# Three written-out orders instead of one for a fused attention kernel, with its loads placed anew

## The chip, the cores and the metric

One Trainium2 chip, one core of it. The metric is the device time of one execution in microseconds (us); lower is better. TensorE (PE) does the matmuls, VectorE (DVE) reductions and element work, ScalarE (ACT) exponentials and copies, GpSimd (POOL) small element work, and SyncE (SP) issues nearly all DMAs.

## The reference, cut to what matters

Four sequences of 1024 rows, 256 wide, with a context of 154 rows each:

```python
x = attention(ln1(x), ln1(x), Wq1, Wkv1, Wo1, bo1) + x        # 16 heads of 16, over 1024 keys
x = attention(ln2(x), context, Wq2, Wkv2, Wo2, bo2) + x       # 16 heads, over 154 keys
x = geglu_ff(ln3(x), Wff1, bff1, Wff2, bff2) + x              # 256 -> 2*1024 -> 256
# second layer: one head, 256 wide, over the 154 context rows
out = softmax((x@Wq.T+bq) @ (ctx@Wk.T+bk).T) @ (ctx@Wv.T+bv) + x
```

## The kernel before, in words

The 4096 rows are cut into NCH = 16 chunks of 256. A chunk goes through five stages, each in another iteration of one software pipeline over n: **pre** (layer norm, q, k and v, letter p, 8 steps) in iteration n = chunk; the self-attention itself (letters M, Q, T, S, V, O, o, u) of chunk n-5; **mid** (Wo1, residual, layer norm, q2; letter m, 9 steps) of chunk n-6; **cross** (the attention over the context; letter c, 36 steps) of chunk n-7; **last** (Wo2, feed-forward, second layer; letter l, 26 steps) of chunk n-8. Iterations 0 to 3 are a head of their own; then run() goes over n = 4 to 20, and walk_end does what is left (mid and cross of chunk 15, cross of 14, last of 13, 14 and 15) by END_ORDER.

Within an iteration the order of all work is a string, ORDER, of 248 letters. Every engine walks the same string by walk() and takes from each letter what that letter's work has for it; so each engine's queue is in the string's order, and engines meet only at semaphores. A letter whose stage doesn't exist in the iteration (l before n = 8, p from n = 16 on) is passed over. SP, too, is only held by its own waits and may be far ahead of TensorE in the string.

The letters that matter here:

- S is half a step of scores (2 matmuls, then one exponential on ACT), V is two steps of probabilities times values (16 matmul records), M is one matmul of 512 columns whose row maximum VectorE reduces; 64, 16 and 64 of them in an iteration. After 16 M's a unit (4 heads) is complete: Q reduces the pairs on VectorE, T turns the result on TensorE (waiting for Q), makes the shift of the exponentials on VectorE, and SP stores it. Units of M run two ahead of those of S. I write T3 for the fourth T, c35 for the last of the 36 steps of c, counting from 0.
- o stores an attention output (SP), u loads the stacks of q and k of a later unit (SP), O copies an output from PSUM (ACT).
- c1 to c12 are maxima of the cross-attention (3 matmuls or 1, and one reduction on VectorE each), c13 turns them, c14 stores the shift (SP), c16 to c35 are scores, exponentials and values. At c25 and c35 SP stores half of its output to DRAM (store_o2).
- The four letters d, i, e, f prepare the last stage of the *next* iteration: d waits until c35's store has landed and loads the softmax denominators (den_c); i inverts them on VectorE, which waits for that load, and SP stores the inverses; e loads the output sums (oT2); f waits for the inverses' landing and loads them broadcast (den2). VectorE multiplies the two in l2, and TensorE projects in l3.
- x loads the q2 stack of the next cross stage; in every fourth iteration (n = 10, 14, 18) k2 and v2 too. TensorE first needs it at c1 of the next iteration.

```python
sp.wait_ge(c_ost, (o + 1) * 32)                  # d, on SP
load_den(1, o2_rows(o))
...
dve.wait_ge(c_den[which], (o + 1) * 16)          # i, on VectorE
nc.vector.reciprocal(den_c[which][:, :], den_c[which][:, :]).then_inc(c_rd[which], 1)
```

In walk_end the letters are c and d (cross of chunks 14 and 15), m (mid of 15), x, y, z (last of 13, 14, 15), and loads: q (the cross stack for d), i j k l (the four load steps for y), r s t u (the same for z).

Of the kernel before, what the change touches and what calls it, by code (L numbers as in the profile page):

```python
# [21 lines left out]
NCH = B * S // CH  # L22
# [34 lines left out]
MAX_LAG, ATT_LAG, MID_LAG, CROSS_LAG, LAST_LAG = 4, 5, 6, 7, 8  # L57
# [3 lines left out]
LEAD = 2  # L61


ORDER = (
    "cMMSSMlSoMSMcSSMlcMSlcVScMM"
    "SmcllVuMSSMucMSMmSSoMmMScSMlQcVTcp"
    "SpcSMMlcSOVMcSMSlSMScVcMpS"
    "SMlVMSpMlcMSucSpMcSMlScMpSMSlcMVM"
    "ScQlSpSTpcScmcMMlcVMcSMlSMcSMOSclmMu"
    "SVVMSMSmcMlSoSMmMScMSlMmMMQSlcVTlcMM"  # L70
    "SlcSMSMOVSMcmSMlSclMSMVxcSdM"
    "SMlSMSMVSMSMSMSiMQeflSVoTVOl"
)


CT_STEPS = 3
# [12 lines left out]
def setup_steps(n, slot):  # L89

    return SETUP_AT.count(SLOTS * (n - MAX_LAG) + slot)
# [4 lines left out]
END_CROSS = dict(c=NCH - 2, d=NCH - 1)  # L96
END_LAST = dict(x=NCH - 3, y=NCH - 2, z=NCH - 1)
END_LOADS = dict(q="d", i="y", j="y", k="y", l="y", r="z", s="z", t="z", u="z")
END_ORDER = "mcxcccccxxccxccmxcmcxccxccccmmcccxccmxccmxxcmxccmcxxcccccxccxqxkxxixddxdddxdjddlxdxdddyydxdddyyxdddyzdddyyddddydddddyddddyyydryyyzystyzzzyyzyyzyuzzzzzzzzzzzzzyzzyyyzzzz"


def in_end(o):
# [26 lines left out]
def xattn_kernel(nc, t, out):  # L129

    ctx = ExitStack()
    with ctx:
# [308 lines left out]
        def walk(n, flags, setup, pre, mid, cross, last, work):  # L441


            has_pre, has_max, has_att, has_mid, has_cross, has_last = flags
            chains = dict(
                p=pre(n) if has_pre else None, m=mid(n - MID_LAG, has_pre) if has_mid else None,
                c=cross(n - CROSS_LAG) if has_cross else None, l=last(n - LAST_LAG) if has_last else None)
            seen = dict.fromkeys(ORDER, 0)
            for letter in ORDER:
                k = seen[letter]  # L450
                seen[letter] += 1
                if letter in work:
                    work[letter](k)
                elif letter in chains and chains[letter] is not None:
                    next(chains[letter])
                if letter == "S" and k % 2:
                    for _ in range(setup_steps(n, k // 2)):
                        next(setup)
            assert all(next(chain, None) is None for chain in chains.values() if chain is not None)

        def walk_end(mid, cross, last, loads=lambda letter: None):
# [4 lines left out]
            chains["m"] = mid(END_MID, False)  # L466
            for letter in END_ORDER:
                if letter in END_LOADS:
# [9 lines left out]
        def _(sp):  # L478
# [266 lines left out]
            def body(n, u, flags, att_before, after):  # L745
# [27 lines left out]
                def for_last(step):  # L773
# [3 lines left out]
                    return load  # L777

                walk(n, flags, setup_work, pre, mid, cross, last, dict(
                    T=store_shift, o=store_unit, u=load_unit, x=load_next_cross, d=for_last(load_last_den),  # L780
                    i=for_last(store_last_inv), e=for_last(load_last), f=for_last(load_last_inv)))
# [19 lines left out]
        def _(pool):  # L801
# [119 lines left out]
            def body(n, u, flags, att_before, after):  # L921
                walk(n, flags, setup_work, pre, mid, cross, last_by(1 - u), {})
# [8 lines left out]
        def _(act):  # L931
# [185 lines left out]
            def body(n, u, flags, att_before, after):  # L1117
                def exp_tile(k):
                    if not flags[2]:
                        return  # L1120
                    step, pair = SLOTS * (n - ATT_LAG) + k // 2, k % 2
                    act.wait_ge(g_s, 2 * step + pair + 1)
                    if step >= PR:
                        act.wait_ge(g_av, step - PR + 1)
                    nc.scalar.activation(probs[:, step % PR, 2 * pair:2 * pair + 2, :].rearrange("p j q -> p (j q)"),  # L1125
                                         ps_s[pair][:, :], ACT.Exp, scale=SCALE).then_inc(g_e, 1)

                def o_copy(k):
                    if not flags[2]:
                        return  # L1130
                    unit = HG * (n - ATT_LAG) + k
                    act.wait_ge(g_av, (unit + 1) * KT)
                    act.wait_ge(g_ost[unit % 2], unit // 2 * 16)
                    nc.scalar.copy(o_sb[:, unit % 2, :], ps_o[:, 0:CH]).then_inc(g_o, 1)

                walk(n, flags, setup_work, pre_by(flags[3]), mid, cross_by(not flags[2]), last, dict(
                    S=exp_tile, O=o_copy))
# [618 lines left out]
```

## Time and profile before

| | |
|---|---|
| median of 3 runs | 1776.59 us (1768.93 to 1783.04) |
| the profiled execution | 1771.07 us |
| its span, first to last instruction | 1769.3 us |
| mean granted clock of TensorE in it | 0.964 |
| TensorE, VectorE, ScalarE busy | 91%, 63%, 56% |
| iterations n = 5 to 20 | 96.5 us to 1592.8 us of the span |
| walk_end | 1592.8 us to 1769.3 us |

A busy TensorE is not one at its peak: a record of 128x256 lasts longer than the time until the next one may start. All times below are from the profiled execution.

### The profile page before, as it was taken

What the parts mean: (1) busy time and instruction counts of PE and PEld (TensorE: products, weight loads), DVE (VectorE), ACT (ScalarE), POOL (GpSimd) and SP (SyncE); (2) the same over time, 40 slices, a digit from 0 to 9 for tenths busy, and PEclk for the clock granted to TensorE, in tenths of its full rate; (3) what the DMA queues carried; (4) which work ended last, traced back from release to release, by engine and by line L of the source; (5) the groups of instructions that cost most, each with busy time, mean ns of one, the idle gap of its engine ahead of it and who ended that gap; (6) DMA issues with size and microseconds to landing.
All of it is one profiled execution on the core that took longest, in us unless ns stands there. A gap on an engine that the chain in (4) does not pass through costs nothing.

```text
span 1769.3 us, 33823 instructions
## 1 busy us (share of the span) xinstructions
PE 1610.6 (91%) x12897; PEld 1027.3 (58%) x12897; DVE 1109.2 (63%) x2221; ACT 988.1 (56%) x2024; POOL 264.9 (15%) x344
## 2 busy tenths in 40 slices
PE   6799999998999899998999899998999899896777
PEld 5444445564757566564756566564656556565566
DVE  4466786757676585857677585857676575824332
ACT  3246667565656466565656565565656556563232
POOL 5200312111111020121111021101010010101000
PEclk9989999999999999999999999999999999998788
DMA  6904243345131312445131321535030412221200
GB/s 186 223 23 132 60 87 82 82 88 122 43 85 52 66 59 62 97 85 117 51 83 50 62 60 55 104 58 116 18 83 26 79 38 48 59 43 46 56 25 13
DMA packets 171647, 129.37 MB, mean 73 GB/s; under 512 B 40751, under 2 KB 161885, under 8 KB 171229
## 3 DMA queue, kind: packets, MB, share of 16 engines
q1 hardware_dynamic: 171421, 127.19, 30.1%
q8 instruction: 102, 1.67, 0.4%
q14 instruction: 60, 0.49, 0.1%
q10 hardware_dynamic: 64, 0.02, 0.0%
HBM read 78.92 MB, written 47.71 MB: 72 GB/s over the span
## 4 chain that ended last, share of the span: by engine, by line
PE 63%; DVE 17%; DMA 10%; issue 3%; ACT 3%; SPq 3%; POOL 0%; DVEq 0%; POOLq 0%; ACTq 0%
PE ps_last L1620 10%; PE ps_max L1675 9%; PE ps_o L1709 9%; PE ps_s L1697 8%; DVE mxh L1346 7%; PE ps_last L1629 6%; DMA o_s<-o_sb 5%; PE ps_pre L1484 4%; PE ps_pre L1492 3%; PE ps_cross L1588 3%; DVE mx L1271 3%; PE ps_cross L1574 2%; DMA den_c<-o_s 2%; DMA den<-o_s 1%; DVE th L1303 1%
## 5 line engine op out<-in xcount | busy, mean ns | idle before, releaser
L1346 DVE TENSOR_REDUCE mxh<-ps_max 128x1 f32<-128x512 f32 x1024 | 661.1, 681 | 195.0 <-PE ps_max L1675 192.6
L1125 ACT ACTIVATE probs<-ps_s 128x512 f32<-128x512 f32 x1024 | 580.8, 598 | 302.4 <-PE ps_s L1697 278.7
L1675 PE MATMUL ps_max<-kst,qst 96*128 96x512 bf16 x1024 | 386.0, 393 | 21.3 <-DVE mxh L1346 11.7
L1697 PE MATMUL ps_s<-qst,kst 98*128 98x256 bf16 x2048 | 386.1, 277 | 6.7 <-ACT probs L1125 3.8
L1709 PE MATMUL ps_o<-probs,vg 128*17 128x256 f32 x4096 | 271.9, 387 | 0.0
L1697 PEld LDWEIGHTS ps_s<-qst,kst 98*128 98x128 bf16 x2048 | 176.7, 99 | 163.8 <-ACT probs L1125 72.6
L1675 PEld LDWEIGHTS ps_max<-kst,qst 96*128 96x128 bf16 x1024 | 96.0, 98 | 159.2 <-DVE mxh L1346 88.8
L1303 DVE SCALAR_TENSOR_TENSOR th<-th,gb 128x256 f32<-128x256 f32 x128 | 67.3, 526 | 178.7 <-ACT gb L1097 178.6
L1709 PEld LDWEIGHTS ps_o<-probs,vg 128*17 128x17 f32 x4096 | 96.5, 97 | 108.3 <-issue 42.0
L1066 ACT ACTIVATE probs<-ps_cross 77x512 f32<-77x512 f32 x224 | 132.6, 592 | 44.2 <-PE ps_cross L1574 44.0
L1620 PE MATMUL ps_last<-y_hi,wff_hi 128*128 128x256 f32 x448 | 141.1, 315 | 7.9 <-DVE hT L1306 7.9
L1620 PE MATMUL ps_last<-y_lo,wff_hi 128*128 128x256 f32 x448 | 126.4, 282 | 0.0
L1620 PE MATMUL ps_last<-y_hi,wff_lo 128*128 128x256 f32 x448 | 125.8, 281 | 0.0
L1629 PE MATMUL ps_last<-wff,hT 128*128 128x256 f32 x480 | 112.8, 380 | 2.0 <-DVE hT L1306 2.0
L1095 ACT ACTIVATE th<-ps_last,b_tanh 128x256 f32<-128x256 f32 x112 | 53.0, 473 | 98.4 <-PE ps_last L1620 97.3
L1620 PEld LDWEIGHTS ps_last<-y_hi,wff_hi 128*128 128x128 f32 x448 | 84.8, 189 | 22.1 <-DVE hT L1306 14.9
L863 POOL TENSOR_TENSOR qk_f<-qk_f,qk_parts 128x512 f32<-128x512 f32 x40 | 46.3, 1158 | 330.3 <-ACT qk_f L1033 167.1
L1629 PEld LDWEIGHTS ps_last<-wff,hT 128*128 128x128 f32 x480 | 87.9, 190 | 13.1 <-DVE hT L1306 2.6
L1574 PE MATMUL ps_cross<-q2st,k2st 98*77 98x256 bf16 x448 | 86.6, 274 | 8.4 <-ACT probs L1066 4.9
L854 POOL TENSOR_SCALAR ve<-mv 128x2 f32<-128x2 f32 x34 | 7.8, 230 | 557.6 <-DVE mv L1209 557.6
L1620 PEld LDWEIGHTS ps_last<-y_lo,wff_hi 128*128 128x128 f32 x448 | 85.0, 190 | 1.0
L1620 PEld LDWEIGHTS ps_last<-y_hi,wff_lo 128*128 128x128 f32 x448 | 85.1, 190 | 0.0
(265 smaller groups left out, 2013.0 us busy)
## 6 DMA issues: line engine op xcount, KB each, us to landing
parts_s<-qk_parts SPq DMA_DIRECT2D x28, 384.0 KB, 3.8
o_s<-o_sb SPq DMA_DIRECT2D x64, 128.0 KB, 2.8
o_s<-o_sb SPq DMA_DIRECT2D x32, 256.0 KB, 3.7
oT<-o_s SPq DMA_DIRECT2D x62, 128.0 KB
den<-o_s SPq DMA_DIRECT2D x62, 128.0 KB
kst<-parts_s SPq DMA_DIRECT2D x16, 384.0 KB, 5.0
kst<-parts_s SPq DMA_DIRECT2D x48, 128.0 KB, 5.9
qst<-parts_s SPq DMA_DIRECT2D x64, 96.0 KB, 2.2
```

The source lines that it names most:

```text
L1066: nc.scalar.activation(probs2[:, h % PR2, :], cross_banks[spare][h % 2][0:CT, :], ACT.Exp, scale=SCALE).then_inc(c_e, 1)
L1125: nc.scalar.activation(probs[:, step % PR, 2 * pair:2 * pair + 2, :].rearrange("p j q -> p (j q)"), ps_s[pair][:, :], ACT.Exp, scale=SCALE ...
L1271: nc.vector.tensor_reduce(mx2[:, h0:h0 + nh, i], cross_max_banks[spare][f % 2][:, 0:nh * CTX].rearrange("p (h n) -> p h n", h=nh), AX_X, A ...
L1303: nc.vector.scalar_tensor_tensor(th[:, m % 2, :], th[:, m % 2, :], 1.0, gb[:, m % 2, :], ALU.add, ALU.mult).then_inc(c_gt, 1)
L1346: nc.vector.tensor_reduce(mxh[:, i // 2, i % 2:i % 2 + 1], ps_max[i % 2][:, :], AX_X, ALU.max).then_inc(g_mx, 1)
L1484: last = mm(bank[:, m * CH:(m + 1) * CH], w[:, k, m * P:(m + 1) * P], y[:, k, :], start=(k == 0), stop=(k == KD - 1))
L1574: last = mm(cross_banks[spare][h % 2][0:CT, a * CH:(a + 1) * CH], k2st[:, at, a * CT:(a + 1) * CT], q2st[:, at, :], start=True, stop=True)
L1620: last = mm(last_banks(o)[m % 2][:, part * CH:(part + 1) * CH], wff1[w][:, k, cols_], y3[y][:, k, :], start=(i == 0), stop=(i == len(terms ...
L1629: last = mm(bank_[:, i * D:(i + 1) * D], hTs[e][:, m, i * P:(i + 1) * P], wff2[:, m, :], start=(m == 0), stop=(m == FM - 1))
L1675: mm(ps_max[i % 2][:, :], qst[0:ROWS, h, q * P:(q + 1) * P], kst[0:ROWS, h, k * 512:(k + 1) * 512], start=True, stop=True).then_inc(g_mt, 1)
L1697: last = mm(ps_s[pair][:, j * CH:(j + 1) * CH], kst[:, h, kt * P:(kt + 1) * P], qst[:, h, :], start=True, stop=True)
L1709: last = mm(ps_o[j * W:j * W + VW, 0:CH], vg[:, g, kt, j * VW:(j + 1) * VW], probs[:, step % PR, j, :], start=(kt == 0), stop=(kt == KT - ...
```

## The change

The one string becomes three: EARLY for n = 4 to 7 (no last stage yet), STEADY for n = 8 to 15 (all stages), LATE for n = 16 to 20 (no pre stage). Each holds the same letters as often as ORDER did, in another order. END_ORDER has the same letters in another order. No instruction is added or removed.

```diff
-ORDER = (
-    "cMMSSMlSoMSMcSSMlcMSlcVScMM"
...
-    "SlcSMSMOVSMcmSMlSclMSMVxcSdM"
-    "SMlSMSMVSMSMSMSiMQeflSVoTVOl"
+EARLY = (
+    "SSMMSMSMMSMSMSMcSVMo"
...
+    "SMlllllcMSmMMcVcSMOSMcmSMSdMlSVlSM"
+    "SlMVMSoSMMoSSMSMMQSSOlVlxTlielflVlll"
+STEADY = (
+    "lMMMSMcSMSMSMScScSMSMc"
...
+    "SclMMVVMMcSmlMSMlMSMclMMlQScSmVTcSSMcmMcl"
+    "SSMVMScSMOlSMmMlcMoSlMSMVSMM"
+    "SVSdMSMSMxSMQSlSSVioTVOefl"
+LATE = (
+    "MMlSSoMSMSMSMSMMSSMcccMl"
...
+    "SScmcMSSMVMmMSlcMSSMlOclSMVMMd"
+    "SxSMlMSSMVMSMlSMSieQVSlfTOoV"
+def order_of(n):
+
+    return EARLY if n < LAST_LAG else STEADY if n < NCH else LATE
-END_ORDER = "mcxcccccxxccxccmxcmcxccxccccmmcccxccmxccmxxcmxccmcxxcccccxccxqxkxxixddxdddxdjddlxdxdddyydxdddyyxdddyzdddyyddddydddddyddddyyydryyyzystyzzzyyzyyzyuzzzzzzzzzzzzzyzzyyyzzzz"
+END_ORDER = "cmcccccccxcxccxccccxcmcxmcxcccxcccccmcmmxxymccxmmxccxzdcxcyqxccxcxxxxxidddddxdjddxddddkdxxldxddyddddyxyddddddddyddydddzdydryyyysytyyzyyzzyyuzyzyzzzzzzzzyzzzzzyzyzyyzzzz"
-            seen = dict.fromkeys(ORDER, 0)
-            for letter in ORDER:
+            seen = dict.fromkeys(order_of(n), 0)
+            for letter in order_of(n):
```

## Rows read from the trace of the kernel before

**Rows 1.** The page: busy time by engine, and TensorE's granted clock in 40 slices.
```profile
PE 1610.6 (91%) x12897; PEld 1027.3 (58%) x12897; DVE 1109.2 (63%) x2221; ACT 988.1 (56%) x2024; POOL 264.9 (15%) x344
...
PEclk9989999999999999999999999999999999998788
```

**Rows 2.** Busy time by stretch: iterations 7, 10, 11, 18 and walk_end; length first.
```profile
core 0: us, PE busy (x) PEld busy (x) DVE busy (x) ACT busy (x) POOL busy (x), PEclk, DMA share, GB/s
...
238.80:314.60 75.80, 70.98 (x630) 37.33 (x629) 54.43 (x107) 50.75 (x100) 13.43 (x17) 0.99 0.27 71
...
514.70:618.60 103.90, 95.45 (x799) 61.92 (x798) 68.63 (x138) 60.41 (x124) 15.77 (x21) 0.98 0.28 67
618.60:716.00 97.40, 94.61 (x799) 62.18 (x798) 67.49 (x138) 60.53 (x124) 16.02 (x21) 0.99 0.23 61
...
1311.60:1411.70 100.10, 90.55 (x770) 56.80 (x769) 64.94 (x132) 56.73 (x117) 9.01 (x13) 0.97 0.26 56
...
1592.80:1769.30 176.50, 134.01 (x815) 102.71 (x814) 60.85 (x135) 53.28 (x121) 16.67 (x25) 0.81 0.13 35
```

**Rows 3.** Who waited for whom, TensorE, 303 to 1506 us: total, times, longest.
```profile
PE ps_max L1683 <- DVE mxq L1354: 40.5, 24, 5.4
```

**Rows 4.** The same view, within iteration 11 (619 to 700 us).
```profile
PE ps_max L1683 <- DVE mxq L1354: 0.8, 1, 0.8
```

**Rows 5.** Timeline of all engines at the end of iteration 10: start, length, idle before.
```profile
612.39 0.59 SPq L616 DMA_DIRECT2D den_c<-o_s  x1
614.45 0.35 DVE L1229 RECIPROCAL den_c<-den_c 128x32 f32<-128x32 f32 x1 [7.03 <-DMA den_c<-o_s]
...
615.39 0.17 DVE L1354 TENSOR_REDUCE mxq<-mxh 128x8 f32<-128x16 f32 x1
...
615.61 0.38 PE L1683 MATMUL ps_max<-ident,mxq 128*8 128x128 f32 x1 [5.40 <-DVE mxq L1354]
```

**Rows 6.** Timeline of SP's issues, ends of iterations 10 and 11.
```profile
599.18 0.33 SPq L660 DMA_DIRECT2D q2st<-q_s  x1
...
603.37 0.39 SPq L696 DMA_DIRECT2D o_s<-o_sb  x1
...
702.62 0.33 SPq L660 DMA_DIRECT2D q2st<-q_s  x1
702.99 2.10 SPq L667 DMA_DIRECT2D q2st<-q_s  x3
705.56 0.38 SPq L696 DMA_DIRECT2D o_s<-o_sb  x1
711.00 0.59 SPq L616 DMA_DIRECT2D den_c<-o_s  x1
```

**Rows 7.** DMA issues: count, KB each, median us from issue to landing.
```profile
o_s<-o_sb SPq DMA_DIRECT2D x64, 128.0 KB, 2.8
o_s<-o_sb SPq DMA_DIRECT2D x32, 256.0 KB, 3.7
...
q2st<-q_s SPq DMA_DIRECT2D x48, 128.0 KB, 5.9
```

**Rows 8.** The chain that ended last, iteration 15 and its end: start, length, what.
```profile
1085.49 0.44 PE ps_s L1697 x4
...
1092.01 1.73 PE ps_last L1629 x8
...
1103.97 0.99 PE ps_o L1709 x16
...
1106.29 4.82 DMA o_s<-o_sb
...
1111.13 2.16 DMA den_c<-o_s
...
1117.33 4.58 DMA den<-o_s
```

**Rows 9.** Busy time by stretch: the first 20 us of iteration 15.
```profile
1019.70:1039.70 20.00, 18.01 (x163) 9.98 (x161) 19.69 (x43) 11.19 (x21) 5.84 (x10) 0.99 0.31 91
```

**Rows 10.** Who waited for whom, TensorE, walk_end (1592.8 to 1769.3 us).
```profile
PE ps_last L1492 <- DVE oT L1234: 6.8, 2, 4.8
...
PE ps_s L1574 <- DMA q2st<-sh_lo: 2.4, 1, 2.4
PE ps_cross L1561 <- DVE mx L1271: 2.1, 1, 2.1
```

More of the change, by code:

```diff
@@ L61 @@
 LEAD = 2
-ORDER = (
-    "cMMSSMlSoMSMcSSMlcMSlcVScMM"
[L66 to L70, printed above, removed]
-    "SlcSMSMOVSMcmSMlSclMSMVxcSdM"
-    "SMlSMSMVSMSMSMSiMQeflSVoTVOl"
-)
+EARLY = (
+    "SSMMSMSMMSMSMSMcSVMo"
+    "SMSMSccSccMScMVMSumcSMMmQScmc"
+    "SVTpcSScuMpMScOVSMScVpSSMcoMcV"
+    "ScMpMSMSMpMcMSSMupMcSMVcMSSMcppQcTVOlc"
+    "SlmMcSMclSMllScMMScSMMcSSmMcV"
+    "SMmScMSMVMScMSMSmlMlulllcSMQVTcS"
+    "SMlllllcMSmMMcVcSMOSMcmSMSdMlSVlSM"
+    "SlMVMSoSMMoSSMSMMQSSOlVlxTlielflVlll"
+)
+STEADY = (
+    "lMMMSMcSMSMSMScScSMSMc"
+    "SlcMVoclSMcMSucSlMMlSVSSmMMSQc"
+    "SVTSlcSMcMlcmVScMMSSmOpplSoSMpcccV"
+    "SMSlSVpMMlSMuMcpScSMMlcpMMlVMMScQSlcpTc"
+    "SSpmcuMSSMclcSMVcSSmMulScOMM"
+    "SclMMVVMMcSmlMSMlMSMclMMlQScSmVTcSSMcmMcl"
+    "SSMVMScSMOlSMmMlcMoSlMSMVSMM"
+    "SVSdMSMSMxSMQSlSSVioTVOefl"
+)
+LATE = (
+    "MMlSSoMSMSMSMSMMSSMcccMl"
+    "SMcluVScMSMclMcMSlVSSMVcQmScST"
+    "SlccSMSoMlSScVMcMSOlScmVMMSlMcVM"
+    "SSlcScMmSSppMSMpcMplpcpSMMppcSl"
+    "SuMcMVQlcSTcSScmMMlcVMMSOuSclSuSc"
+    "SMMSVlmMcMlMMmScSlSMMSVMcMmSoMlMQcSlVTcM"
+    "SScmcMSSMVMmMSlcMSSMlOclSMVMMd"
+    "SxSMlMSSMVMSMlSMSieQVSlfTOoV"
+)
+def order_of(n):
+    return EARLY if n < LAST_LAG else STEADY if n < NCH else LATE
 CT_STEPS = 3
```

## The prediction

> **What bounds the kernel now.** I read the page first: TensorE is busy 91% of the span, VectorE 63%, and the granted clock is full except in the last four slices [rows 1]. So the bound is TensorE's queue and what holds it up, and the prize is its idle time, some 159 us of 1769.3. Then I cut the span at the first S of each iteration and read busy time by stretch. Iterations with all stages last 103.9 and 97.4 us with the same work and nearly the same busy TensorE (95.5 and 94.6), in turns, even ones longer; LATE-type iteration 18 has 100.1 against 90.6 busy [rows 2]. The reader is to see that the difference is waiting, and that it alternates. The view of waits names it: T, which turns the maxima, waits for Q on VectorE, 40.5 us in 24 waits, the longest 5.4 [rows 3]. No other wait of TensorE in that stretch holds 6 us in all.
>
> These are two kinds. Twelve are the T0 of iterations 8 to 19, 0.8 us each [rows 4], because Q0 stands just ahead of T0 behind VectorE's backlog: 12 x 0.8 = 9.7. The other 30.8 us are T3 at the iteration's end (the same view at each of the twelve ends gives 2.5, 1.2, 5.4, 0.5, 3.3, 0.2, 4.8, none, 3.8, 1.4, 5.2, 0.5 for iterations 8 to 19, and 2.0 for 7). The timeline of iteration 10 says why: VectorE idles 7.03 us in i, which waits for den_c; Q3 is behind i, so it comes at 615.39, and T3 behind that with 5.40 idle [rows 5]. And i is late because of SP's queue: x's ten loads start at 599.18, c35's store is behind them at 603.37, d may issue only when that store has landed, at 612.39, nine microseconds on [rows 5, 6]. In iteration 11, with four loads ahead (702.62), the store takes 705.56 to 711.00, 5.4 us [rows 6]. That is the alternation, in part: ten loads in 10, 14 and 18, the stacks of k of a new sequence in 8, 12 and 16.
>
> **The ends of iterations, STEADY.** Two moves. First, d stands ahead of x, so c35's store no longer has loads ahead of it. Second, i stands behind Q3 and V14, directly ahead of T3, and d to i is longer.
>
> PE time of a letter, from the chain: two S are 0.44, so S (and M) is 0.22; V is 0.99; an eight-record step of l is 1.73 [rows 8]. From the start of c35 to i, ORDER has 8 S, 7 M, a V, l23 and c35: 15 x 0.22 + 0.99 + 0.44 + 0.95 = 5.7 us. STEADY has 11 S, 9 M, 3 V, l23, l24 and c35: 4.4 + 3.0 + 0.4 + 1.7 + 1.0 = 10.5 us. The chain needs c35 0.95, the ACT copy 0.4, the store's landing, den_c's 2.16 with issue [rows 8] and 0.4 for the gaps. The store alone has no row of its own; bounds are 2.8 (128 KB stores) and 4.82 (iteration 15, four loads ahead) [rows 7, 8]; the median of all 256 KB stores is 3.7 [rows 7], half of them with loads ahead, and I take 3.2. Sum 7.1 us, at most 8.7, under 10.5. So i doesn't wait, and even if it did, Q3 is already done: what is late next would be M0 of the next iteration, which needs T3's shift from VectorE. T3 to M0 is one V (0.99) against 1.0 us for the turn and two small VectorE operations, even. All T3 waits of 8 to 15 go: 2.5 + 1.2 + 5.4 + 0.5 + 3.3 + 0.2 + 4.8 + 0 = 18.
>
> **LATE and EARLY.** In LATE i is ahead of Q3 but c35 to i is 9 M, 8 S, 2 V, l23, l24 and c35, 8.9 us against 7.1: 1.8 us of slack, and nil with the upper bound. T3 waits of 16 to 19 are 3.8 + 1.4 + 5.2 + 0.5 = 11, but Q3 to T3 is now V, S and no l24, 1.2 us, and I leave 0.5 each: -9. The order is also made for the missing p: iteration 18 has 9.6 us not busy, 4.4 with T3's 5.2 taken off, where ORDER bunches S, M and c after p's letters drop out. I take -1 for each of five, bounds +1 and -2: -5. In EARLY, iteration 7's T3 wait of 2.0 goes, because i is behind T3. For the rest of 4 to 7 VectorE is the tight engine (54.4 busy of 75.8 with TensorE at 71.0 [rows 2]) and I see no gain there, -2 in all, bounds +3 and -6.
>
> **What the moves cost.** (1) x is now issued after d, thus after the landing of c35's store: about 0.95 + 0.4 + 3.2 + 0.7 = 5.3 us after c35's start. Four loads are there 2 + 5.9 us after the first issue [rows 7], 13.2 after c35; TensorE reaches the next c1 after 11.6 (to the end) and 2.6, so 14.2 us in STEADY, 14.8 in LATE. Covered by 1 us. The ten loads of 10, 14 and 18 have no landing row that I quote but took up the queue from 599.18 to about 611 (the store behind them landed by 612.39 [rows 5, 6]): 11 to 13 us, so 16.3 to 18.3, 2 to 4 us late for c1, three times, less what iterations are longer than their pure PE time (6 us, so half a microsecond in this stretch): +6, bounds 0 and +12. (2) The inverses' store stands behind x's loads, and SP has o3 and T3's shift store ahead of e and f. f is issued some 5 us after T3 and takes 4.58 [rows 8], 9.7; l2 comes at 1.2 + 6.3 us of PE time, stretched by VectorE, about 8.3. In the first 20 us of an iteration VectorE is busy 19.69 [rows 9], so a wait in its queue costs its full length: +1 each for eight. But before, f landed at 1121.9 (1117.33 + 4.58), 5.7 us into iteration 16, with l2 already waiting, so the difference may be nil. I book 0, bounds +8 and -8. (3) That first stretch holds the same reductions in STEADY as in ORDER (12 of c and as many M, within two), so it stays at its 20 us. (4) u1 moves from before S12 to behind the first unit, so SP no longer stands there with T0's shift and m's loads behind it; nobody waits for these now, and the gain is nil.
>
> One rule of the skill speaks against (1) and (2). Rows 6 show the store of 256 KB take 9.0 us behind ten loads and 5.4 behind four. The Trainium skill, "DMA: Bandwidth & Descriptors", section "Queues, rings and completion order", says that an issuing engine has one ring on each DMA engine and that its descriptors are consumed in ring order, so whatever is put behind x's loads waits for them; the trace agrees. By that rule the change doesn't remove the queueing but hands it from den_c's path to that of the inverses, which is the second rival below.
>
> **walk_end**, 176.5 us with TensorE at 134.0 busy and a mean clock of 0.81 [rows 2]. The letters take the same PE time. x3 waited 4.8 us for x's inverses (the longest of L1492's 6.8 [rows 10]); END_ORDER now has c8 to c12 ahead of it, which fill that wait, and the turn c13 follows at once instead of behind two stalls of 2.1 and 2.4 [rows 10]. The first exponentials of cross 14 come some 8 us earlier, of which I count half, because afterwards c21 to c25 stand alone and go at ACT's pace. The load q is ahead of c35's store instead of behind it (1.9 us wait at d1), and y3 is behind d16 to d20 (1.9). z3 has 15 us behind d35 rather than 9 (2.0). Against that, d13 to d16 has lost y3 as its cover (+2), and heads 5 to 8 of d are no longer mixed with the feed-forward (+2). Sum -4 - 1.9 - 1.9 - 2.0 + 4 = -6; with a little less time at half clock, -8. Bounds +4 and -22.
>
> **The sum**, against the profiled execution's 1771.07 (span 1769.3 and 1.8 around it): -18 - 9 - 5 - 2 + 6 - 8 = -36, so 1735. The median shown is 5.5 us above that execution, inside a spread of 14; I put the forecast at 1736.
>
> **The clock** is the one place where a rule gives another result. In this trace it falls to half (1.2 GHz) for one or two short spells right behind the long T3 waits, in iterations that then last no longer: iteration 11 begins so and has 97.4 us [rows 2], and VectorE bounds that stretch anyway [rows 9]. So I book nothing for it in the main loop.
>
> **The rivals.**
> A. *Less idle also gives back clock time.* If the spells at half clock behind the T3 waits (some 37 us in seven) cost what TensorE loses in them, half, then 19 us more: 1717. Against it: odd iterations, which begin with the spell, are the short ones. The Trainium skill, "TensorE: Matmul & The Clock Gate", names as penalty throttled time times one minus the ratio, which is this half; the trace of iteration 11 speaks against it. A better walk_end (-22) gives the same place.
> B. *The wait moves to f and x.* VectorE waits at l2, or TensorE at c1, 1.3 us in each of 13 iterations instead of nil: +17 and 1753. For it: both slacks are about a microsecond, and VectorE is full there. Decides: f's landing against l2.
> C. *Slower.* If c35's store still takes its 4.8 to 5.4 us, x is issued 2 us later and lands 1 to 2 us after c1 each time, 6 us after it in 10, 14 and 18, and the inverses' path is behind those loads, so l2 stalls by 3 more: (2 + 1.5) x 10 + 9 x 3 = 62 against 42 of gains, 1791. It decides from a store of about 5 us on. Against it: nothing stands ahead of that store now but small ones.
> D. *The strings of their own do nothing*: STEADY alone, -18 + 4, 1757.
>
> **Chances.** Forecast (1725 to 1748) 0.57, A 0.14, B 0.15, D 0.09, C 0.05. The range holds A's upper part, B and D: 1710 to 1764. Within 1% of 1776.6, 1758.8 to 1794.4, is what a measurement of this kernel tells from no change. Faster: the forecast, A, most of B, half of D, 0.86, less some for unseen stalls: 0.84. Same 0.12, slower 0.04.
>
> **What would show it.** The profile after should have L1683's wait down from 40.5 to some 12 to 15 us; d's issue (L616) ahead of q2st's (L660) and some 3 us after c35's store; iterations 8 to 15 at 96 to 99 us without alternation, 16 to 19 at 92 to 95; walk_end at 165 to 172. A new row "PE ps_cross L1556 <- DMA q2st" would be cost (1), more time in "DVE oT L1234 <- DMA den" cost (2), and either above 15 us makes the forecast wrong upwards; iterations of 94 us without a spell at half clock, downwards.

## The result, and the profile after

The changed kernel takes 1709.53 us (median of 4 runs, 1707.72 to 1712.48), against 1776.09 before (median of 4, one more than the table ahead of the prediction had); the ratio is 0.9627, with a 95% interval of 0.9586 to 0.9668. Run again beside the kernel before (a_again, below) it was 1709.47 and 0.9649 (0.9623 to 0.9675). The forecast was 1736, and its range ended at 1710. The direction held and the main waits went as described; the size was short by 26 us between forecast and median, by 23 between the 36 us booked and the 58.6 between the two profiles.

The page of the profiled execution (1712.48 us, span 1710.7), against [rows 1]:

```profile
PE 1609.0 (94%) x12897; PEld 1019.8 (60%) x12897; DVE 1120.2 (65%) x2221; ACT 996.5 (58%) x2024; POOL 269.4 (16%) x344
...
PEclk9989999999999999999999999999999999997789
```

TensorE is busy for nearly the same time, 1609.0 us against 1610.6; 57.0 of the 58.6 us of span that went were its idle time. By stretch, with the same columns as [rows 2]: iterations 7, 10, 11, 18, 19 and walk_end.

```profile
236.60:310.30 73.70, 70.75 (x636) 37.72 (x633) 55.32 (x108) 51.32 (x100) 13.45 (x17) 1.00 0.37 82
504.40:601.10 96.70, 94.67 (x799) 61.49 (x798) 68.90 (x138) 61.11 (x124) 16.59 (x21) 1.00 0.28 67
601.10:697.80 96.70, 94.67 (x799) 61.48 (x798) 68.90 (x138) 61.10 (x124) 16.20 (x21) 1.00 0.26 67
...
1272.60:1366.20 93.60, 90.27 (x770) 56.53 (x769) 65.68 (x132) 57.05 (x118) 9.05 (x13) 1.00 0.22 54
1366.20:1460.50 94.30, 90.36 (x771) 56.61 (x770) 65.87 (x132) 57.15 (x118) 9.06 (x13) 1.00 0.23 56
1546.60:1710.70 164.10, 137.02 (x800) 101.60 (x798) 61.10 (x132) 53.65 (x121) 17.21 (x25) 0.81 0.15 39
```

Iterations 10 and 11 are alike now, 96.7 us, where they were 103.9 and 97.4, and the clock is at 1.00. The last S ends at 1546.8, so walk_end proper is 163.9 us. Cut the same way all along, the time went here:

| | before | after | gained | booked |
|---|---|---|---|---|
| up to the end of iteration 7 | 314.6 | 310.3 | 4.3 | 2 |
| iterations 8 to 15 | 801.6 | 773.5 | 28.1 | 18, less 4 of the 6 for x |
| iterations 16 to 20 | 476.6 | 463.0 | 13.6 | 14, less 2 of the 6 |
| walk_end | 176.5 | 163.9 | 12.6 | 8 |

Who waited for whom, TensorE, 301 to 1460 us, to be set beside [rows 3]: T's wait was 40.5 us in 24 and is 1.1 in 4. The prediction's own sign for it was 12 to 15 us, because it took the T0 waits (0.8 us each) to stay; they are all but gone too.

```profile
PE ps_last L1647 <- DVE hT L1333: 7.0, 16, 0.6
PE ps_max L1702 <- DVE mxh L1373: 6.1, 16, 0.6
...
PE ps_max L1710 <- DVE mxq L1381: 1.1, 4, 0.3
```

SP's issues at the end of iteration 10, beside [rows 5, 6] (L723 is c35's store, L643 d, L687 to L703 x, L647 the inverses' store, L656 f). These are nine loads, four of q2, four of k2 and one of v2; the prediction says ten, which is a miscount:

```profile
588.72 0.38 SPq L723 DMA_DIRECT2D o_s<-o_sb  x1
...
590.91 0.59 SPq L643 DMA_DIRECT2D den_c<-o_s  x1
591.60 0.53 SPq L687 DMA_DIRECT2D q2st<-q_s  x1
...
596.19 0.39 SPq L703 DMA_DIRECT2D v<-v_s  x1
598.39 0.61 SPq L647 DMA_DIRECT2D o_s<-den_c  x1
...
603.51 1.19 SPq L656 DMA_DIRECT2D den<-o_s  x2
```

The store lands 2.2 us after its issue (588.72 to 590.91), where it took 9.0; the median of the 32 such stores fell from 3.7 [rows 7] to:

```profile
o_s<-o_sb SPq DMA_DIRECT2D x32, 256.0 KB, 2.2
```

And the inverses' store now is the one behind the nine loads: issued at 598.39, it lets f go at 603.51, 5.1 us later. The queueing was handed on, as the prediction said it might be (its second rival). What it costs is the subject of half of the experiments.

### The profile page after: what moved, and what is told of

Its sections match the earlier page's. It is cut to its first block, busy times and chain, and to the rows that moved or that the text cites. A ratio compares the mean times of both kernels' runs of the same rounds, so it can differ in the third digit from the quotient of the medians.

```text
span 1710.7 us, 33819 instructions
## 1 busy us (share of the span) xinstructions
PE 1609.0 (94%) x12897; PEld 1019.8 (60%) x12897; DVE 1120.2 (65%) x2221; ACT 996.5 (58%) x2024; POOL 269.4 (16%) x344
## 4 chain that ended last, share of the span: by engine, by line
PE 71%; DVE 18%; ACT 5%; issue 3%; DMA 2%; SPq 1%; POOL 0%; DVEq 0%; ACTq 0%; POOLq 0%
PE ps_o L1736 11%; PE ps_max L1702 10%; PE ps_last L1647 9%; PE ps_s L1724 9%; DVE mxh L1373 8%; PE ps_last L1656 6%; PE ps_cross L1615 4%; PE ps_pre L1511 3%; PE ps_pre L1519 3%; DVE mx L1298 3%; PE ps_cross L1601 2%; PE ps_last L1685 2%; DVE th L1330 1%; ACT probs L1152 1%; PE ps_last L1519 1%
## 5 line engine op out<-in xcount | busy, mean ns | idle before, releaser
L1702 PE MATMUL ps_max<-kst,qst 96*128 96x512 bf16 x1024 | 363.4, 385 | 21.5 <-DVE mxh L1373 15.2
L1724 PE MATMUL ps_s<-qst,kst 98*128 98x256 bf16 x2048 | 371.6, 274 | 6.5 <-ACT probs L1152 4.9
L1724 PEld LDWEIGHTS ps_s<-qst,kst 98*128 98x128 bf16 x2048 | 171.7, 98 | 155.7 <-ACT probs L1152 57.9
L1736 PEld LDWEIGHTS ps_o<-probs,vg 128*17 128x17 f32 x4096 | 94.1, 96 | 112.2 <-issue 48.3
```

The source lines that it names most:

```text
L1702: mm(ps_max[i % 2][:, :], qst[0:ROWS, h, q * P:(q + 1) * P], kst[0:ROWS, h, k * 512:(k + 1) * 512], start=True, stop=True).then_inc(g_mt, 1)
L1724: last = mm(ps_s[pair][:, j * CH:(j + 1) * CH], kst[:, h, kt * P:(kt + 1) * P], qst[:, h, :], start=True, stop=True)
L1736: last = mm(ps_o[j * W:j * W + VW, 0:CH], vg[:, g, kt, j * VW:(j + 1) * VW], probs[:, step % PR, j, :], start=(kt == 0), stop=(kt == KT - ...
```

## The experiments

Times are beside runs of the kernel before on the same chip, as ratios with 95% intervals; "the changed kernel" is 0.9627 and 0.9649 by this measure. A thousandth is 1.8 us. Single executions vary: 31 of the kernel before on one chip lie between 1758.1 and 1779.8 us, and in the profiles with the old END_ORDER walk_end alone takes 173.0 to 184.9 us. So iterations are compared by stretch.

### One letter, or two, in the old string

**b_x**: x behind d, nothing else.

```diff
-    "SlcSMSMOVSMcmSMlSclMSMVxcSdM"
+    "SlcSMSMOVSMcmSMlSclMSMVcSdxM"
```

> The kernel before with one letter moved: x (the loads of the next cross stage) stands directly behind d instead of ahead of c35. Theory Q (the wait at T3 is queueing: x's loads ahead of c35's store): the store lands in 2.2 to 3.2 us instead of 5.4 to 9, den_c is there about 7 us after c35, i stands 5.7 us of TensorE's time behind c35 and waits 1 us or so, and the T waits of 40.5 us fall to 13 to 18; time 22 to 32 us less. Theory L (what counts is that i stands ahead of Q3): the wait at T3 stays at 2 us or more an iteration, time 0 to 10 us less.

Measured: 0.9953 (0.9926 to 0.998), 8 to 9 us less. Theory Q is right about the wait and wrong about the time, which falls into Theory L's range. T3 never waits; the 10.6 us left are T0's. But (waits of TensorE, 301 to 1600 us):

```profile
PE ps_cross L1556 <- DVE mx L1271: 13.2, 12, 2.4
PE ps_max L1683 <- DVE mxq L1354: 10.6, 13, 0.8
...
PE ps_cross L1556 <- DMA k2st<-k_s: 8.6, 3, 3.3
```

Three times c1 waits some 3 us for x's nine loads, and the iterations with that wait are the long ones (11, 15 and 19; iterations 10, 11 and 12 by stretch):

```profile
511.30:608.90 97.60, 94.06 (x799) 61.82 (x798) 68.65 (x138) 60.46 (x125) 15.73 (x21) 1.00 0.24 62
608.90:711.30 102.40, 95.67 (x799) 62.56 (x798) 68.75 (x138) 60.38 (x125) 15.72 (x21) 0.98 0.28 67
711.30:809.30 98.00, 93.97 (x798) 61.77 (x797) 68.56 (x137) 60.36 (x125) 15.73 (x21) 1.00 0.47 98
```

This is cost (1) of the prediction, to the size of it, in ORDER. In the changed kernel it is nil: from c35's store to the next iteration there are 12.4 us (588.72 to 601.1) and here 9.7 (599.2 to 608.9), and the same loads land 11 to 12 us after x's first issue.

Cost (2) is there as well. The inverses' store (L620), now behind x's loads, keeps f (L629) back for 7.9 us, and VectorE waits at l2 for f's load, which in the kernel before came to 1.7 us in the same window (301 to 1600 us):

```profile
607.37 0.61 SPq L620 DMA_DIRECT2D o_s<-den_c  x1
...
615.23 1.19 SPq L629 DMA_DIRECT2D den<-o_s  x2
```
```profile
DVE oT L1234 <- DMA den<-o_s: 13.9, 11, 2.9
```

The maxima of c stand behind l2, and TensorE's wait for them (the 13.2 us above) was 5.9 in the kernel before. So some 30 us of T3 waits were paid for with 8.6 us at c1 and 7 us at the maxima, and with smaller ones.

**b_i**: i, e, f behind Q3 and V14, the loads as they were.

```diff
-    "SMlSMSMVSMSMSMSiMQeflSVoTVOl"
+    "SMlSMSMVSMSMSMSMQlSViefoTVOl"
```

> The kernel before with i, e and f moved from ahead of Q3 to directly ahead of T3's store, loads as they were. Theory L: the T3 waits are gone and 25 to 30 us with them. Theory Q: VectorE stands at i until the same moment (den_c landed 14 us after c35 in iteration 10), so the wait only moves from T3 to the first M, which needs T3's shift; 4 to 12 us less, and a new wait of TensorE at the first M or c, of 1 to 4 us in even iterations.

Measured: 0.9974 (0.9949 to 0.9999), 3 to 5 us less. Theory Q again: T3 doesn't wait, and M0, which needs T3's shift from the engine that stands in i, does. TensorE, then VectorE, 301 to 1600 us (that the first row is M0 is read from the order of the letters; the view names no releaser):

```profile
PE ps_max L1675 <- issue: 14.2, 6, 4.6
```
```profile
DVE den_c L1229 <- DMA den_c<-o_s: 19.9, 10, 5.1
```

**b_ix**: both.

> Both moves in the kernel before. If these two letters carry the change in the main loop, the T3 waits are gone altogether (30.8 us) and T0's 0.8 each stay: iterations 8 to 15 last 97 to 98 us without alternation, time 30 to 38 us less than before. If the clock spells behind the T3 waits cost time too, they are gone as well and it is 38 to 45 us less. The rest of the 59 us then belongs to the other letters (T0, walk_end, LATE).

Measured: 0.9972 (0.994 to 1.0004). Iterations 8 to 10 and 12 to 14 last 97.6 to 99.6 us, 11, 15 and 19 101.9, 102.2 and 98.5, with 8.2 us of c1's waits for k2st and 15.7 us of l2's for f. The expectation of 30 us or more was badly out: with both moves 4 to 5 us are gained, 11 at most by the interval, since the time comes back at the next iteration's beginning.

```profile
DVE oT L1234 <- DMA den<-o_s: 15.7, 11, 2.7
```

### What the spell at half clock costs

**b_fill**: the kernel before, with extra matmuls in T3's wait.

```diff
+                    if k == HG - 1 and n in (10, 12, 14, 16, 18):
+                        pe.wait_ge(c_q2f, n - MID_LAG + 1)
+                        for _ in range(8):
+                            mm(ps_pre[:, 0:CH], wq1[:, 0, 0:P], wq1[:, 1, :], start=True, stop=True)
                     pe.wait_ge(g_mp, unit + 1)
```

> The kernel before with eight extra matmuls (128x256, float32, 3.5 us in all, result not used) on TensorE just ahead of T3 in iterations 10, 12, 14, 16 and 18, where it waits 3.3 to 5.4 us anyway. Theory K (the spell at half clock behind the wait costs time): the clock stays at full in the five places, and each gives 1.5 to 2 us: 7 to 10 us less. Theory N (the spell costs nothing, since VectorE bounds the stretch, as the prediction had it): the spells go and the time stays within 2 us, or is up to 1 us longer.

Measured: 0.9973 (0.995 to 0.9996). 1004 to 1024 us, over the T3 of iteration 14, in the kernel before and then in this one; the granted clock is the eighth number:

```profile
1004.00:1024.00 20.00, 14.85 (x118) 7.57 (x120) 11.04 (x22) 8.97 (x18) 0.13 (x1) 0.91 0.68 123
```
```profile
1004.00:1024.00 20.00, 18.49 (x149) 10.48 (x147) 12.43 (x25) 9.38 (x18) 0.98 (x2) 1.00 0.64 125
```

The spells of those five places are gone, and iterations 10 to 19 take 984.1 us instead of 991.7, about 1.5 us for each; the medians give 5 us, 1 for each. So theory K, at the small end: the clock behind a T3 wait cost something, which the prediction booked at nothing, and the whole of it is of the order of 10 us in seven places. The Trainium skill, "TensorE: Matmul & The Clock Gate", in its table of terms, has the penalty as the throttled time times one minus the clock ratio, which is half of it here. The five spells of the kernel before last 27 us together by the granted clock, which would be 13.7 us by that rule, an estimate; the runs give 5 to 8.

This run also shows ORDER's iterations nearly bare. Taking off the extra matmuls (3.8 us from the first of them to T3) and what T3 still waits, iterations 10 to 15 last 97.1 to 97.5 us, and 16 to 19 last 93.6 to 94.1.

### The string cut in two

ORDER and STEADY hold the same letters in their first 136, so each beginning fits each end.

**h_tail**: ORDER's beginning and STEADY's end in iterations 8 to 15 of the changed kernel.

> The changed kernel, with the first 136 letters of STEADY (up to the end of the third fifth) those of ORDER; the last 112 letters, with c35, d, x, i and T3, stay STEADY's (the two strings hold the same letters up to there, so this is a clean cut). Theory E (the gain of iterations 8 to 15 is made at their end): T3 waits stay away, T0's 0.8 us come back: iterations of 97.5 us without alternation, whole kernel 5 to 9 us slower than the changed one (1715 to 1719 beside it at 1710). Theory H (the later c1 and l2 at the beginning are needed too, as in b_x, where 11 and 15 lost 4.5 us): iterations 11 and 15 last over 100 us, 12 to 18 us slower.

Measured: 0.9888 (0.9853 to 0.9923), 1749.5 us, 40 more than the changed kernel and more than either theory had. All eight iterations last 100.3 to 103.5 us, T3 doesn't wait, and c1 hardly waits for k2st. The waits of TensorE and of VectorE, 301 to 1020 us:

```profile
PE ps_cross L1583 <- DVE mx L1298: 25.0, 7, 5.0
...
PE ps_cross L1583 <- DMA k2st<-k_s: 1.1, 1, 1.1
```
```profile
DVE oT L1261 <- DMA den<-o_s: 22.5, 7, 4.6
```

VectorE stands in l2 for f's load in every iteration, 3.2 us, with the maxima of c behind it. In the changed kernel the same line (301 to 1080 us) reads:

```profile
DVE oT L1261 <- DMA den<-o_s: 0.4, 1, 0.4
```

**h_head**: STEADY's beginning and ORDER's end.

> The changed kernel, with the first 136 letters of STEADY kept and the last 112 those of ORDER (x ahead of c35, i ahead of Q3). Theory E: T3 waits of 18 us and the clock's spells come back in iterations 8 to 15, T0's 0.8 stay away: 18 to 25 us slower than the changed kernel (1728 to 1735). Theory H: the later l2 and c1 take part of that up, 8 to 14 us slower.

Measured: 0.9813 (0.9791 to 0.9835), 1738.3 us, 29 more than the changed kernel. Theory E's mechanism, and over its time (18 to 25). The T3 waits are back as they were (2.6, 1.3, 5.4, 0.6, 3.3, 0, 5.0, 0) though T0 waits nowhere:

```profile
PE ps_max L1710 <- DVE mxq L1381: 18.1, 6, 5.4
```

Iterations 8 to 15 take 805.5 us here and 813.7 in h_tail, against 801.6 before and 773.5 in the changed kernel. So each half by itself keeps nothing of the 28 us.

### l2's place alone

**a_l2**: the changed kernel, l1 and l2 of STEADY earlier.

```diff
-    "lMMMSMcSMSMSMScScSMSMc"
-    "SlcMVoclSMcMSuc..."
+    "lMMMSMcSMSMSMSllcScSMSMc"
+    "ScMVocSMcMSuc..."
```

> The changed kernel with l1 and l2 of STEADY moved up from 4.7 and 6.3 us of TensorE's time behind the iteration's start to about 3, ORDER's place; nothing else. Theory F (the place of l2 against f's landing decides, which the prediction gave as cost 2 and booked at nil): VectorE waits about 3 us for den2 in each iteration, with its reductions behind it, and each of 8 to 15 lasts 3 to 5 us more, 25 to 38 us in all, as in h_tail. Rival G (h_tail lost because of the other 134 letters of ORDER's beginning, above all T0 and c1 to c12): at most 10 us more.

Measured: 0.9918 (0.989 to 0.9945), 1755.8 us: 46 us more for two letters, of which l2 is one multiplication of 0.69 us that VectorE now meets some 3 us earlier. Theory F, beyond its range. Iterations 8 to 15 last 101.3 to 103.2 us. TensorE and then VectorE, 301 to 1080 us:

```profile
PE ps_cross L1583 <- DVE mx L1298: 34.8, 8, 5.3
```
```profile
DVE oT L1261 <- DMA den<-o_s: 34.6, 8, 5.2
```

The wait of one engine is the other's, within 0.2 us: in this stretch nothing buffers between them. Iterations 8 to 15 take 45 us more than the changed kernel's; the 10 us that the waits leave over go with the clock, which is at half for 51 us in eight spells, one in each iteration, where the changed kernel has none. That they are the clock's price is not tested by itself.

### x back in front

**a_x**: the changed kernel with x ahead of c35 in STEADY and LATE.

```diff
-"...SMOlSMmMlcMoSlMSMVSMMSVSdMSMSMxSMQSlSSVioTVOefl"
+"...SMOlSMmMlxcMoSlMSMVSMMSVSdMSMSMSMQSlSSVioTVOefl"
```

> The changed kernel with x back directly ahead of c35 in STEADY and LATE. If the loads ahead of c35's store are what made i late, den_c lands 9 to 14 us after c35 instead of 6; i stands 10.5 us (STEADY) and 8.9 us (LATE) behind it, so waits appear in iterations 10, 14 and 18 (3 to 5 us each) and of 0 to 1 us in the others: 9 to 16 us more. If the place of i alone has cured the wait: within 3 us.

Measured: 0.9792 (0.9765 to 0.982), 1734.0 us, 25 more. The first theory, though larger: VectorE waits for den_c 11.1 us in five iterations (the longest 3.9) up to 1080 us. In STEADY, where i is behind Q3, T3 doesn't wait for it; as in b_i, M of TensorE stands instead. T3 of 16 to 18, where i is ahead of Q3, waits 2.7, 0.8 and 4.4. VectorE, then TensorE, 301 to 1080 us:

```profile
DVE den_c L1256 <- DMA den_c<-o_s: 11.1, 5, 3.9
```
```profile
PE ps_max L1702 <- issue: 8.9, 12, 3.2
```

### Later l in the old string

**b_xl**: b_x with l1, l2, l3, l4 later.

```diff
-    "cMMSSMlSoMSMcSSMlcMSlcVScMMSmcllVuMSSMucMSMm..."
+    "cMMSSMlSoMSMcSSMcMScVScMMSmcllVuMSlSMuclMSMm..."
```

> The kernel before with x behind d, as in b_x, and the first steps of l later: l1 and l2 from 2.8 and 3.5 us to 6.1, l3 from 6.1 to 7.5, l4 from 7.9 to 10.4. If what a few loads' places leave over is only c1's wait for k2st (3.3 us in 11, 15, 19) it is 2 to 5 us faster than b_x (0.992 to 0.994 of the kernel before). If l2's waits were most of b_x's remaining stalls it is 8 to 15 us faster than b_x (0.987 to 0.991). The changed kernel's 0.965 is then still 20 us or more away, which belongs to the other letters of the strings and to END_ORDER.

Measured: 1.0062 (1.0032 to 1.0092), slower than the kernel before; both expectations fell. T0 doesn't wait any more, but the first quarter of an iteration (from its first S to its seventeenth) is 19.4 us in iteration 10 instead of b_x's 17.2, and the waits of TensorE from 301 us on are:

```profile
PE ps_max L1675 <- DVE mxh L1346: 27.1, 36, 1.6
PE ps_last L1492 <- DVE oT L1234: 11.1, 13, 1.4
PE ps_cross L1556 <- DMA k2st<-k_s: 8.9, 3, 3.8
```

VectorE no longer waits for f. It isn't fuller either; it idles more, and the clock has spells at half, 16 of them and 75 us in all, where b_x has 4 with 17 us. The first 20 us of iteration 14, in b_x and here:

```profile
907.20:927.20 20.00, 17.00 (x147) 9.44 (x145) 18.79 (x42) 10.31 (x20) 5.09 (x8) 1.00 0.40 105
```
```profile
918.70:938.70 20.00, 16.90 (x136) 9.12 (x134) 17.47 (x37) 9.38 (x18) 5.53 (x8) 0.91 0.37 101
```

In the new order l3's projection on TensorE stands five letters behind l2's multiplication instead of ten and waits for it (the 11.1 us). How the waits of M (27.1 us, 5.2 in b_x) and the clock share the rest is not separated. T0's 0.8 us vanished here while the iteration got longer, so its going is by itself no sign of a gain.

### The strings of their own

**a_one**: STEADY in all iterations.

```diff
-    return EARLY if n < LAST_LAG else STEADY if n < NCH else LATE
+    return STEADY
```

> The changed kernel with STEADY in all iterations, 4 to 20: EARLY and LATE are not used. If the strings of their own carry nothing (rival D) it is within 3 us of the changed kernel: b_x had iterations 16 to 18 at 94.6, 95.0 and 93.9 us with ORDER's letters, LATE has 95.1, 93.7 and 93.7. If they carry what the prediction booked beside the T3 waits (5 for LATE, 2 for EARLY) it is 5 to 8 us slower.

Measured: 0.9877 (0.9853 to 0.9902), 1749.7 us, 40 more; neither. Of the profile's 37 us, 31 are in iterations 4 to 7 (which end at 341.3 instead of 310.3 us, with as much VectorE work), and 6 in 16 to 20.

```profile
0.00:341.30 341.30, 287.85 (x1932) 151.67 (x1933) 202.30 (x378) 171.02 (x328) 78.04 (x88) 0.93 0.41 103
```

In the changed kernel the same work reads:

```profile
0.00:310.30 310.30, 271.48 (x1931) 147.81 (x1932) 201.44 (x378) 169.52 (x328) 78.09 (x88) 0.97 0.45 113
```

TensorE needs 16 us more for the same instructions at a lower granted clock, and idles 15 us more.

**a_ol**: ORDER in iterations 4 to 7 and 16 to 20, STEADY between.

> The changed kernel with the old ORDER in iterations 4 to 7 and 16 to 20, STEADY and END_ORDER as they are. EARLY: 2 to 4 us (iterations 4 to 7 took 310 us in the changed kernel and 313 in b_x). LATE: the T3 waits of 16 to 18 come back (10 us), and iteration 16 begins with ORDER's early l2 behind STEADY's late f (3 to 5 us). 14 to 20 us slower than the changed kernel.

Measured: 0.9813 (0.9755 to 0.9872), 1735.1 us, 26 more. Iterations 4 to 7 end 5 us later, 16 to 20 take 475.9 us instead of 463.0 (T3 waits of 1.6, 0, 4.6, 0.4), which accounts for 18. So LATE is worth about 13 us against the old string and 6 against STEADY; EARLY 5 against the old one and 31 against STEADY. That STEADY's p, m and c stand too close there without l's letters between would explain the 31; it was not tested.

### walk_end

**a_oldend**: the changed kernel with the old END_ORDER.

> The changed kernel with END_ORDER as before. walk_end took 163.9 us in the changed kernel, and 176.5, 173.5, 183.6, 174.5 and 184.9 in the five profiled with the old END_ORDER, so if END_ORDER is the cause: 10 to 20 us slower, and x3 waits 4 us or more again. If walk_end gained from what comes ahead of it (LATE's earlier loads, another phase of the clock), it is within 5 us.

Measured: 0.9752 (0.9717 to 0.9788), 1726.2 us, 17 more; walk_end 176.3 us. END_ORDER it is. (Over all profiles walk_end takes 173.0 to 184.9 us with the old one and 157.0 to 164.1 with the new one.)

**b_endnew**: b_xl with the new END_ORDER.

> b_xl with the new END_ORDER. In the changed kernel the old END_ORDER cost 17 us (1726 against 1709.5). If END_ORDER's gain doesn't hang on LATE, this is 12 to 18 us faster than b_xl; if it needs LATE's earlier loads at the end of iteration 20, 5 us or less.

Measured: 0.9999 (0.9976 to 1.0023), 7 us less than b_xl by the medians and 11 by the ratios; walk_end 164.1 against 173.0. Between the two expectations: a gain of 7 to 11 us doesn't need LATE; whether the rest of the 17 does is open.

**a_x3**, **a_q**, **a_y3**: one placement each put back in the new END_ORDER.

```diff
-END_ORDER = "cmcccccccxcxccxccccx..."        # a_x3
+END_ORDER = "cmcccccccxxxxccccccc..."
-... "cxcyqxccxcxxxxxi" ...                   # a_q
+... "cxcyxccxcqxxxxxi" ...
-... "xldxddydddd" ...                        # a_y3
+... "xldxdyydddd" ...
```

> The changed kernel with x0 to x3 of END_ORDER moved back ahead of c8 (x0, x1, x2, x3, then c8 to c14). If the wait of TensorE at x3 and the later turn c13 are what END_ORDER removed, walk_end takes 5 to 10 us more (the prediction had 4 for it); if END_ORDER's gain is in the middle (q ahead of c35, y3 behind d16 to d20), within 2 us.

> The changed kernel with the letter q of END_ORDER (the load of cross 15's q2 stack) back behind c35, where SP first waits for c35's output copy. d1 came 1.8 us after x18's end in the changed kernel's order instead of 3.8: if q's place is that difference, d1 waits 2 us again and walk_end takes 2 to 4 us more; if the load lands under x15 to x18 anyway, no difference.

> The changed kernel with y2 and y3 moved back ahead of d16 in END_ORDER. In the old order y2's multiplication stood behind x24's result and TensorE waited 1.9 us at y3 with all of d16 to d35 behind it; in the new one d16 to d20 fill that time. If this carries the middle part of walk_end's gain, it takes 3 to 6 us more; if the fill is what matters less than the order of d against y later on, under 2 us.

Measured: 0.9673 (0.9623 to 0.9723), 0.965 (0.9616 to 0.9683) and 0.9667 (0.9629 to 0.9705), against 0.9627 and 0.9649; walk_end 163.1, 160.0 and 163.4 us. By the medians none of the three is worth more than 3 us, and none can be told from nothing; the intervals of the ratios are too wide to exclude 5 us and more. In a_x3 c16 does come 4 us later (19.1 against 15.6 and 14.6 us into walk_end), and 35 us further on nothing is left of that: d13 starts at 67.1 against 67.8 and 67.2.

**a_warm**: extra matmuls in walk_end's waits.

```diff
+            def warm(times):
+                for _ in range(times):
+                    mm(ps_max[1][:, :], qst[0:ROWS, 0, 0:P], kst[0:ROWS, 0, 0:512], start=True, stop=True)
                         last.then_inc(c_mt, 1)
+                        warm(spare)                # behind each of c1 to c12
...
+                    warm(5 * spare)                # behind c13
```

> The changed kernel with extra matmuls (96x512, bf16, 0.2 us each, result not used) in walk_end's two cross stages: one behind each of c1 to c12 and five behind c13, where TensorE waits for VectorE or the shift's DMA. 34 of them, 7.3 us at full clock, nearly all of it in waits. If the spells at half clock in walk_end (64 us in the changed kernel) come from those waits and cost time, the clock there rises from 0.81 to 0.9 or more and the time falls by 8 to 20 us. If not, 0 to 5 us more.

Measured: 0.9639 (0.9617 to 0.966), 1707.7 us. The stretch at half clock in walk_end falls from 58 to 61 us (a_again and the changed kernel) to 38, and the granted clock rises from 0.81 to:

```profile
1545.70:1706.20 160.50, 135.79 (x832) 100.73 (x832) 60.73 (x132) 53.69 (x121) 16.93 (x25) 0.88 0.14 40
```

and the time changes by nothing that can be told from the changed kernel's. If such time cost half of itself, that would have been 10 us. So what bounds walk_end is, as far as this goes, its dependences and not the clock; a walk_end with no spell at half clock was not run.

**a_again**, the changed kernel beside a_l2, a_x and a_warm:

> The changed kernel once more, beside the other three, to compare them on the same chip: 1705 to 1714 us, iterations 8 to 15 at 96.7, walk_end at 160 to 166.

Measured: 1709.47 us, 0.9649 (0.9623 to 0.9675).

## Why the prediction was right in kind and short in size

**Right.** The T3 waits and their cause (x's loads ahead of c35's store) are as described: b_x alone removes them, b_i alone moves them to M0, h_head brings them back, and so does a_x where i is ahead of Q3 (LATE). The landing of the store, booked at 3.2 us, was 2.2. i's slack was enough. LATE was booked at 14 (before its share of x's cost) and gave 13.6, 13 by a_ol.

**LATE's number is luck in part.** It was booked as 9 of T3 waits and 5 for an order made for the missing p. The waits were worth their full 10.9, and the rest is about what two spells at half clock would give. The 5 are not there: with the T3 waits filled (b_fill) ORDER's own iterations 16 to 19 last 93.6 to 94.1 us, and LATE's 95.1, 93.7, 93.7 and 94.3. The prediction also left out two steps of l in LATE, l22 between c35 and i and l25 between Q3 and T3; both add slack, and no T3 of LATE waits.

**The step that failed is the sum of "What the moves cost" for iterations 8 to 15.** There the prediction has 18 us of T3 waits, 4 of cost (1) taken off, and nothing else: 14 against 28. Three terms were mis-sized, and by the figures below they make up the missing 14: some 4, 5 and 5 us.

- *Cost (1)*, +6 with bounds 0 and 12, was in truth nil. The mechanism is real, 8.6 us in three waits in b_x, but in STEADY c35 is further from the next c1. I had 14.2 us of pure TensorE time from c35's start to c1 and added only half a microsecond for waits; in the trace of the changed kernel it is 16.5 (587.2 to 603.7). The last of k2's loads landed at 602.6, 15.4 us after that start, where I had 16.3 to 18.3 for the whole. So it is covered by 1 us.
- *The clock*, booked at nothing, is 1 to 2 us per spell by b_fill, four spells in 8 to 15: some 5 us. Rival A had the sign right and at 19 us for seven spells about twice the size.
- *"That first stretch stays at its 20 us"*, and with it T0's waits: an iteration of ORDER without T3 waits and without the spells lasts 97.1 to 97.5 us (b_fill), STEADY's 96.7. That is 0.4 to 0.8 us each, some 5 in all. (The 97.6 to 98.2 of b_x still hold its waits at l2.) It is about the size of the T0 wait, which STEADY doesn't have, but which letters do it is not separated; b_xl shows that it isn't l's steps alone.

**Cost (2) was booked at nil and is nil, but not for the reason given.** The prediction said that l2 perhaps waited as much before as after. It hardly waits in either (1.7 us in three waits before, 0.4 in one in STEADY). What happened in between is larger: f is issued 4 us later against the iteration's start (616.90 against 618.6 before, 603.51 against 601.1), and only because l2 stands at 6.3 us of TensorE's time instead of 3.5 does this cost nothing. With l2 at its old place VectorE waits 3 to 5 us in every iteration, and the whole kernel loses 40 to 46 us (h_tail, a_l2). This was the largest price in the case, and rival B's mechanism. Its decision point (f's landing against l2) was named, but the prediction had no figure for what l2's new place was worth; its +1 an iteration was a wait at the new place, and it didn't count the clock behind such a wait.

**walk_end** was booked at 8 and gave 12.6 in the profile, 17 by a_oldend. Of the placements behind "-4 - 1.9 - 1.9 - 2.0 + 4" three were put back, and each alone costs 3 us or less by the medians; z3's 2.0 was not tested. So the runs don't bear out that sum of separate waits; which combination gives the 12 to 17 us stays open. The first exponentials of cross 14 did come 8.7 us earlier (15.6 us into walk_end against 24.3), but a_x3 takes 3.5 us of that back and costs 3 us at most by its median, with nothing left of the delay at d13. What the trace shows is only where the lead grows: x18 is 4.9 us earlier than before, d13 10.2, z3 8.0 and z24 10.8.

**Rival D**, the strings of their own do nothing: false; they are worth 18 of the 59 us against the old string by the stretches of a_ol, 26 us by its median. In LATE, though, it is the placement of x and i that pays, as far as the b_fill figures above tell.

**The base.** The profiled execution of before was 5 us under its median and that of the changed kernel 3 over; 58.6 us between the two profiles are 63 to 67 between medians. That and the missing 23 us put the result half a microsecond below a range whose lower end was drawn for rival A alone.

## What to carry to other kernels

In a software pipeline whose order is written by hand, the wait that the profile names is worth what it says only if the transfers behind it still arrive in time at their own consumer: follow each moved load to the instruction that needs it, in the next iteration too, and ask what is queued behind that one. Here one letter (b_x) removed 30 us of named waits and gained 9, and two steps placed 3 us too early (a_l2) cost 46. Where an engine is full for a stretch, as VectorE is at an iteration's beginning [rows 9], a wait in its queue can cost its full length on the engine that depends on it: 34.6 us on VectorE were 34.8 on TensorE.

## What was not expected of the hardware

A 16 KB store behind nine loads (1.4 MB) took 5.1 us (598.39 to 603.51) and in b_x 7.9 us (607.37 to 615.23), where the median of all such stores is 1.8. A 256 KB store with no loads ahead of it took 2.2 us, and 9.0 behind the nine. In these rows what stood ahead mattered more than the size. And keeping the clock up by extra matmuls was worth 1 to 1.5 us per spell in the main loop but nothing measurable in walk_end, where 20 us less at half clock raised the granted clock from 0.81 to 0.88.

```profile
o_s<-den_c SPq DMA_DIRECT2D x32, 16.0 KB, 1.8
```
